# GRU scan: the r gate's product is taken from `zh` and `new` apart, the n and z gates keep `h`

## The reference, cut to what matters

```python
def cell(h, x):
    gi = x @ W_ih + b_ih
    gh = h @ W_hh + b_hh
    i_r, i_z, i_n = jnp.split(gi, 3, axis=-1)
    h_r, h_z, h_n = jnp.split(gh, 3, axis=-1)
    r = jax.nn.sigmoid(i_r + h_r)
    z = jax.nn.sigmoid(i_z + h_z)
    n = jnp.tanh(i_n + r * h_n)
    h_new = (1.0 - z) * n + z * h
    return (h_new, h_new)
_, hs = jax.lax.scan(cell, initial_state, xs)   # 128 steps, one after the other
```

## Time and profile before

| what | us |
|---|---|
| median of 3 runs | 1871.96 |
| lowest and highest | 1869.98, 1874.99 |
| the profiled execution's own time | 1866.16 |
| its span on the core | 1864.4 |
| mean granted TensorE clock over it | 0.765 |

### The profile page before, as it was taken

The page is one execution under the profiler, slowest core; times in us unless marked ns, Lnnn a source line. Parts: engine busy times, 40 slices in busy tenths (PEclk is TensorE's granted clock), DMA queues, the critical chain, the costliest instruction groups (busy, mean ns, idle before and its releaser), DMA issues. The chain is left out here.

```text
span 1864.4 us, 46760 instructions
## 1 busy us (share of the span) xinstructions
PE 1385.8 (74%) x16570; PEld 1089.6 (58%) x16570; DVE 1318.3 (71%) x6934; ACT 712.3 (38%) x2888; POOL 304.6 (16%) x568
## 2 busy tenths in 40 slices
PE   6898865555555545455469999999999579999975
PEld 4376633333333333333258888888888257777764
DVE  4357779999999999999665655555555446676654
ACT  4658822222222222222433434333433454444332
POOL 1025511111111111111131111111111211111110
PEclk9979975555555555555679999999999889899855
DMA  3000000000000000000210100100000130000000
GB/s 120 0 1 2 2 1 2 2 2 2 2 2 2 2 2 2 2 2 2 96 51 1 35 4 14 35 18 1 1 1 1 46 79 3 3 9 8 14 14 14
DMA packets 15201, 27.96 MB, mean 15 GB/s; under 512 B 1692, under 2 KB 9464, under 8 KB 14584
## 3 DMA queue, kind: packets, MB, share of 16 engines
q1 hardware_dynamic: 14528, 22.83, 3.7%
q0 software_dynamic: 272, 2.10, 0.6%
q10 hardware_dynamic: 168, 0.04, 0.0%
HBM read 20.77 MB, written 4.19 MB: 13 GB/s over the span
## 5 line engine op out<-in xcount | busy, mean ns | idle before, releaser
L773 PE MATMUL bank<-s_tanh_hi,coup_hi 128*128 128x16 f16 x2048 | 140.9, 179 | 317.1 <-ACT s_tanh_hi L764 317.1
L773 PEld LDWEIGHTS bank<-s_tanh_hi,coup_hi 128*128 128x128 f16 x2048 | 94.4, 107 | 364.3 <-ACT s_tanh_hi L764 364.3
L1085 ACT ACTIVATE prob<-bank,neg_max 128x128 f32<-128x128 f32 x256 | 90.7, 366 | 215.5 <-DVE neg_max L1134 215.5
L764 ACT ACTIVATE s_tanh_hi<-s_s 128x32 f16<-128x32 f32 x256 | 58.9, 230 | 231.6 <-DVE s_s L665 231.6
L773 PE MATMUL bank<-s_tanh_lo,coup_hi 128*128 128x16 f16 x2048 | 140.1, 179 | 0.8 <-DVE s_tanh_lo L660 0.2
L1199 POOL TENSOR_TENSOR prob<-prob,inv 128x512 f32<-128x512 f32 x64 | 66.7, 1042 | 426.3 <-DVE inv L1165 426.3
L773 PE MATMUL bank<-s_tanh_hi,coup_lo 128*128 128x16 f16 x2048 | 130.0, 174 | 0.0
L752 POOL TENSOR_SCALAR s_p_scaled<-s_p 128x32 f32<-128x32 f32 x128 | 37.0, 289 | 565.5 <-DVE s_p L731 544.4
L975 PE MATMUL bank<-x_hi,w_hi 128*128 128x512 f32 x256 | 111.4, 435 | 22.9 <-DVE w_lo L1114 21.2
L773 PEld LDWEIGHTS bank<-s_tanh_lo,coup_hi 128*128 128x128 f16 x2048 | 93.6, 106 | 33.5 <-DVE s_tanh_lo L660 0.7
L1415 PE MATMUL bank<-h_hi,w_h_hi 128*128 128x16 f16 x1536 | 91.2, 172 | 21.5 <-DVE h_hi L1633 21.3
(11 more groups left out here) (277 smaller groups left out, 4286.1 us busy)
## 6 DMA issues: line engine op xcount, KB each, us to landing
w_stage<-in_L_cond_qkv_w_dram SPq DMA_DIRECT2D x12, 512.0 KB, 4.9
x_tok<-in_x_dram SPq DMA_DIRECT2D x4, 512.0 KB, 5.7
ow_stage<-in_L_cond_out_w_dram SPq DMA_DIRECT2D x4, 512.0 KB, 5.4
x_in<-x SPq DMA_DIRECT2D x1, 2048.0 KB, 12.0
stage_area<-in_L_cond_ffn_w_dram SPq DMA_DIRECT2D x2, 1024.0 KB, 6.6
x<-x_in POOLq DMA_DIRECT2D x1, 2048.0 KB, 16.5
out_dram<-stage_area SPq DMA_DIRECT2D x64, 32.0 KB, 1.6
ada_w<-in_L_cond_ada_w_dram SPq DMA_DIRECT2D x1, 1536.0 KB, 12.3
```

What stands on the lines that cost most here:

```text
L764: A.activation(th_hi[:, :], s, ACT.Tanh, scale=scale).then_inc(hi_ready, 1)
L773: ins = nc.tensor.matmul(coupled[:, B * m:B * m + B], w[:, o:o + P], th[:, B * c:B * c + B], start=(first and c == 0 and m == 0), stop=(la ...
L1085: last = A.activation(prob[:, grp % 2, h, :], bank[2 + grp % 2][:, T * h:T * h + T], ACT.Exp, bias=neg_max[:, grp % 2, h:h + 1], accum_out ...
```

## The change

The new state is h = 0.5 zh + new, so the r gate's product is W h = (0.5 W) zh + W new. The change takes it from these two apart, in six groups instead of three: 0.5 W high and low with the high part of `zh`, W high and low with the high part of `new`, 0.5 W high with the low part of `zh`, and W high with the low part of `new`. Each has a wait of its own. The groups of n and z follow as before, from `h_hi` and `h_lo`; the second group of n now stands ahead of the wait for `h_lo`. VectorE makes four more tiles a step (`zh_hi`, `new_hi`, `zh_lo`, `new_lo`; n_hi and n_lo in the code), and POOL halves the r weights once, before the scan. The first step takes r from h as before.

```diff
@@ TensorE, in the loop over s
+                if s == 0:
+                    pe.wait_ge(hhi_ready, 1)
+                    product(RB, 0, w_hh, h_hi, False)
+                    product(RB, 0, w_hl, h_hi, False)
+                    pe.wait_ge(hlo_ready, 1)
+                    product(RB, 0, w_hh, h_lo, True).then_inc(r_full, 1)
+                    pe.wait_ge(wr_made, 2)
+                else:
+                    pe.wait_ge(zhh_ready, s)
+                    product(RB, 0, w_rh, zh_hi, False)
+                    product(RB, 0, w_rl, zh_hi, False)
+                    pe.wait_ge(nhi_ready, s)
+                    product(RB, 0, w_hh, n_hi, False)
+                    product(RB, 0, w_hl, n_hi, False)
+                    pe.wait_ge(zhl_ready, s)
+                    product(RB, 0, w_rh, zh_lo, False)
+                    pe.wait_ge(nlo_ready, s)
+                    product(RB, 0, w_hh, n_lo, True).then_inc(r_full, 1)
                 pe.wait_ge(hhi_ready, s + 1)
-                product(RB, 0, w_hh, h_hi, False)
-                product(RB, 0, w_hl, h_hi, False)
                 product(NBK, 2, w_hh, h_hi, False)
+                product(NBK, 2, w_hl, h_hi, False)
                 pe.wait_ge(hlo_ready, s + 1)
-                product(RB, 0, w_hh, h_lo, True).then_inc(r_full, 1)
-                product(NBK, 2, w_hl, h_hi, False)
                 product(NBK, 2, w_hh, h_lo, True).then_inc(n_full, 1)
@@ VectorE, in the loop over s
                 STT(zh[:, :], tz[:, :], 1.0, h32[s % 2][:, :], ADD, MUL).then_inc(zh_ready, 1)
+                if s + 1 < T:
+                    STT(zh_hi[:, :], tz[:, :], 1.0, h32[s % 2][:, :], ADD, MUL).then_inc(zhh_ready, 1)
                 dve.wait_ge(keep_ready, s + 1)
                 dve.wait_ge(cand_ready, s + 1)
+                if s + 1 < T:
+                    V.tensor_tensor(n_hi[:, :], cand[:, :], keep[:, :], MUL).then_inc(nhi_ready, 1)
                 V.tensor_tensor(new[:, :], cand[:, :], keep[:, :], MUL).then_inc(new_ready, 1)
                 dve.wait_ge(zh_ready, s + 1)
+                if s + 1 < T:
+                    dve.wait_ge(zhh_ready, s + 1)
+                    V.tensor_tensor(zh_lo[:, :], zh[:, :], zh_hi[:, :], SUB).then_inc(zhl_ready, 1)
+                    dve.wait_ge(nhi_ready, s + 1)
                 dve.wait_ge(new_ready, s + 1)
+                if s + 1 < T:
+                    V.tensor_tensor(n_lo[:, :], new[:, :], n_hi[:, :], SUB).then_inc(nlo_ready, 1)
@@ POOL, ahead of its loop over s
+            pool.wait_ge(gw_made, 2 * C)
+            G.tensor_scalar(w_rh[:, :, :], w_hh[:, :, 0:D], 0.5, None, MUL).then_inc(wr_made, 1)
+            G.tensor_scalar(w_rl[:, :, :], w_hl[:, :, 0:D], 0.5, None, MUL).then_inc(wr_made, 1)
```

More of the change, by code:

```diff
@@ L1243, in ffn_gru @@
     h_hi, h_lo = sb("h_hi", [P, W], F16), sb("h_lo", [P, W], F16)
+    w_rh, w_rl = sb("w_r_hi", [P, C, D], F16), sb("w_r_lo", [P, C, D], F16)
+    zh_hi, zh_lo, n_hi, n_lo = (sb(n, [P, W], F16) for n in ("zh_hi", "zh_lo", "new_hi", "new_lo"))
     tr, tz = sb("r3", [P, W]), sb("z3", [P, W])
@@ L1267, in ffn_gru @@
     added, init = sem("added"), sem("init3")
+    wr_made, zhh_ready, zhl_ready, nhi_ready, nlo_ready = (
+        sem(n) for n in ("wr_made", "zhh_ready", "zhl_ready", "nhi_ready", "nlo_ready"))
     bank = g.bank
```

## The result

| what | before | after |
|---|---|---|
| median, us | 1872.22 | 1889.30 |
| lowest and highest, us | 1869.98, 1874.99 | 1887.80, 1890.43 |
| ratio, 95% interval | | 1.009, 1.0078 to 1.0102 |
| span of the profiled execution, us | 1864.4 | 1888.3 |
| recurrent steps, first `new` to last, us | 313.2 | 331.1 |

The change made the kernel 17.1 us slower. The two profiled spans lie 23.9 us apart; 17.8 us of that is the scan, and 6.0 us had gathered before it (the first `new` starts at 1540.2 and at 1546.2), in stages that the change doesn't touch. The profiled execution of before was itself 6 us under its median.

A forecast was written before the change was run, and what follows sets the result against it. The scan was taken as bound by the step's chain in 69 steps and by TensorE's issue in 57. Terms 17.1 + 0.6 + 2.3 + 2.2 = 22.2 us gave a median of 1894 us, forecast's own range 1888 to 1900, overall 1882 to 1908.

The forecast's parts named there:

- The unwaited steps: 57 scan steps where TensorE never waited: 12 more matmuls of 25 ns add 0.30 us each, 17.1 us.
- The steps without side work: Last 32 scan steps: earlier r unused, z product ends 0.02 us later, adding 0.6 us in all.
- cand stands behind ACT's z: In the steps without side work, cand waits behind ACT's z, so the early r has nobody to use it.
- The waiting steps with side work: 37 scan steps: 2.3 us for TensorE's products ending later plus 2.2 us for longer VectorE operations.
- the part for TensorE: In the 37 waiting steps with side work, products end 0.03 to 0.20 us later: 2.3 us.
- The part for VectorE: In 20 of those 37 steps a 512-column operation delays `rhn`: 0.24 us in 9, 0.12 in 11, net 2.2 us.
- Cheap edits: POOL's halving of the weights, its later add and ACT's earlier r: nothing, unless the halving took over 20 us.
- r did not decide: Rival, chance 0.06: ACT's r sets the waiting steps, each 0.28 us shorter, 19.3 us saved; 1870 us.
- The clock did not hold better: Rival, chance 0.10: added matmuls keep TensorE's clock up in two slow scan stretches, saving 7.8 us; 1886 us.
- VectorE's operations cost: Rival, chance 0.12: four operations ahead of `h_lo` cost 0.19 us each, or their waits cost time; 14 us more, 1908 us.

The follow-up runs named there:

- the zeros: Kernel before, with three groups (12 matmuls) of zero weights added to r's bank in every step but the first: 1890.06 us, ratio 1.0108.
- the four groups: Changed kernel without r's two groups of low weights, so r is taken from four groups instead of six: 1878.15 us, ratio 1.0044 to the kernel before.
- the run without the low part: Changed kernel with the groups of `h_lo` left out of n and z, while VectorE still makes `h_lo`: 1870.67 us in one execution.

## Why the prediction was right

The time was forecast at 1894 us with 1888 to 1900 around it, and came at 1889.3: the mechanism held, the sum was 5 us too large.

*The unwaited steps.* The term was 57 x 0.30 = 17.1 us, and it is the one that was mis-sized. From one `new` to the next there are 127 distances; the 58 in which no wait for `h_hi` fell gave 12.6 us. In the first 16 steps the price was right, 0.30 us in the mean, and the zeros and the four groups show it to be that of the matmuls. In the 43 others it was 0.19 us in the mean. Eight of these had been as long as the chain, 2.30 or 2.31 us, and grew by 0.10 us on average (0.07 to 0.13), though no wait for `h_hi` was seen in them. And a few with little side work differ as in the runs above: steps 22 and 57 were 0.7 us shorter than before, step 61 was 0.9 us longer.

The prediction also counted the gap on the wrong row. The 69 waits of the earlier trace rows are those of the weight loads (PEld). The matmuls themselves waited less often in the same stretch of the kernel before:

```profile
PE bank L1415 <- DVE h_hi L1633: 21.3, 46, 0.8
```

In the other 23 the weight load waited while an earlier matmul was still running, and hardly any gap was left to fill. Counted from one injection of r's gates to the next, TensorE's idle time was under 0.03 us in 74 of the 94 steps before the stretch without side work, 20 of them among the 69. These 74 gave 17.6 us, 0.30 in the median; the other 20 gave 0.9 us.

*The steps without side work.* Forecast was +0.02 us, measured -0.02 us a step (-1.0 us over 32). `h_lo` came at +0.89 against +0.91, and the first matmul of `h_lo` at +1.14 against +1.16. But "cand stands behind ACT's z" was the wrong step: I took from the earlier trace rows that cand follows z by its 0.20 us, when cand was waiting for `pre` there (0.22 us behind its start, and 0.23 now). Now that `pre` is early, cand starts 0.13 us after z, while z still runs (1842.07 and 1842.20). What takes its place is VectorE's list, and in it `zh_hi`, which I had priced at nothing: it fits exactly, and it is the last thing before `new_hi`. The two errors hid one another by luck, since the sum along VectorE (0.23 + 0.09 + 0.11 + 0.10 = 0.53 us) happens to be that along ACT (0.54).

*The waiting steps with side work.* 4.5 us were forecast for 37 of them, and the 37 distances with such a wait gave 6.2 us. What was too low is the part for TensorE: ten of them took 0.29 to 0.37 us, the full price and more. The part for VectorE was slightly high: the 9 with a longer operation came 0.19 us longer in the median (0.24 forecast), those with a shorter one 0.08 (0.12). The prediction had read the 0.74 us from `y_gated` to `rhn` as that operation's time. But in the same step of the kernel before `rhn` (1741.00) came 0.30 us behind ACT's r, as it does in the earlier trace rows (0.29 us):

```profile
1740.70 0.20 ACT L1526 ACTIVATE r<-bank 128x32 f32<-128x32 f32 x1 [1.33 <-PE bank L1415]
```

In the changed kernel, where neither r nor n holds it any more, it follows `y_gated` by 0.66 us:

```profile
1762.40 0.19 DVE L1669 TENSOR_TENSOR h_lo<-h,h_hi 128x32 f16<-128x32 f32 x1
1762.51 0.75 DVE L1585 SCALAR_TENSOR_TENSOR y_gated<-bank,vec,ada 128x512 f32<-128x512 f32 x1
1763.17 0.18 DVE L1636 SCALAR_TENSOR_TENSOR rhn<-r,bank 128x32 f32<-128x32 f32 x1
...
1763.94 0.19 DVE L1650 TENSOR_TENSOR new_hi<-cand,keep 128x32 f16<-128x32 f32 x1
```

From `rhn` to the next start it is 0.77 us, as forecast (0.78), and the step takes 2.44 us, not 2.54.

The three parts make 12.6 + 6.2 - 1.0 = 17.8 us where 22.2 were forecast: one term 4.5 us too large, one 1.7 too small, one 1.6 too large. That the second went the other way brought the total closer, and that was luck.

*Cheap edits.* POOL halved the weights in 1.5 and 1.7 us and then idled 21.7 us: nothing, as said.

*The rivals.* r did not decide; the run without the low part shows that it would, by some 0.2 us, if n and z did not wait for `h_lo`. The clock did not hold better over the scan, 0.83 against 0.82, though it did in some of its stretches and not in others. VectorE's operations cost 0.10 us apiece in their queue, not 0.19.

## What to carry to other kernels

A wait on an engine can only be traded for work on it in the iterations where the engine really waits; here TensorE had no gap in 74 of some 126 steps, and there the 12 matmuls cost 0.30 us in the median. So count, over all iterations, in how many the matmuls, and not only their weight loads, wait for the operand that a change brings forward, and make the change in those alone. And before you bring one of several operands forward, look which of its fellows comes last: r was ready 0.26 us earlier, and its reader waited for n.

## What the runs showed of the hardware

- Two ACT operations overlap in the changed kernel: cand starts 0.13 us after z begins, with z lasting 0.20 us. That agrees in kind with the Trainium skill (ScalarE: Activation LUTs, What ACT_TABLE_LOAD costs), which has back-to-back activations overlap by some 93 ns; here it is 0.07 us. VectorE's operations of 128x32 start 0.10 us apart here at 0.19 us each, unless one needs the one in front: then 0.29 us (`zh_hi` 1850.45 to `zh_lo` 1850.74).
- More matmuls did not raise TensorE's clock in the last stretch. It is busy 61.09 of 71.2 us there in the changed kernel, where it was 49.25 of 72.6 before, and the granted clock is 0.50 in both: 1.2 GHz. The Trainium skill (TensorE: Matmul & The Clock Gate, Why this matters for your kernels) speaks of keeping the engine busy, without idle gaps; here it was idle for (71.20 - 61.09) / 31 = 0.33 us a step instead of 0.75, and these rows do not show the clock rising with that.

The row of the changed kernel (stretch, length, each engine's busy us and count, granted clock, DMA):

```profile
1804.00:1875.20 71.20, 61.09 (x1665) 52.76 (x1661) 50.87 (x369) 18.46 (x97) 8.38 (x31) 0.50 0.05 11
```
